# Attention denominators inverted on gpsimd, as a power of minus one, in place of VectorE's reciprocal

## The reference, cut to what matters

```python
scores = einsum('bmhd,bnhd->bhmn', q, k) / sqrt(2)        # head width 2
scores = where(scores >= 0, scores, 0.2 * scores)
beta = softmax(scores, axis=-1)
out = einsum('bhmn,bnhd->bmhd', beta, v)                  # value width 16
x = xn + (gamma * out + xn) + experts(xn)                 # 12 MLP experts, top 2 of 16
```

## Time and profile before

| | us |
|---|---|
| median of 3 runs (941.28 to 942.41) | 942.19 |
| profiled execution, first to last instruction | 940.0 |
| DVE busy in it | 735.3 (78%) |
| PE busy | 861.2 (92%) |
| ACT busy | 691.3 (74%) |
| POOL busy | 601.5 (64%) |
| first attention stretch (about) | 127 to 365 |
| experts (about) | 365 to 541 |
| second attention stretch (about) | 541 to 936 |

### The profile page before, as it was taken

One profiled execution on the slowest core, in us unless ns is written; L12 is line 12 of the kernel. 1 busy time (PEld: TensorE's weight loads), 2 busy tenths in 40 slices (PEclk: granted clock), 3 DMA queues, 4 the chain that ended last, 5 costly groups with the idle time before them and its releaser, 6 DMA issues. The chain is left out here.

```text
span 940.0 us, 20061 instructions
## 1 busy us (share of the span) xinstructions
PE 861.2 (92%) x7499; PEld 348.9 (37%) x7500; DVE 735.3 (78%) x859; ACT 691.3 (74%) x811; POOL 601.5 (64%) x610
## 2 busy tenths in 40 slices
PE   0688269999999999999999999999999999999997
PEld 0444112222222224776867732222222222222222
DVE  5788889999999994101011099999999999999996
ACT  0578888888888887444453568888888888888886
POOL 3355247777777663999999226657567575765782
PEclk9999659999999999999999999999999999999999
DMA  7833101111111112233242210102112111210202
GB/s 214 303 66 74 32 27 33 51 40 51 47 27 36 25 38 88 90 121 116 93 138 71 94 44 22 40 19 59 36 25 59 25 36 29 70 29 13 69 18 55
DMA packets 71225, 59.36 MB, mean 63 GB/s; under 512 B 33770, under 2 KB 58178, under 8 KB 71136
## 3 DMA queue, kind: packets, MB, share of 16 engines
q1 hardware_dynamic: 61520, 48.06, 17.6%
q0 software_dynamic: 8192, 9.37, 3.6%
q10 hardware_dynamic: 1424, 0.76, 0.3%
HBM read 31.58 MB, written 30.02 MB: 66 GB/s over the span
## 5 line engine op out<-in xcount | busy, mean ns | idle before, releaser
L1133 DVE TENSOR_SCALAR ps<-ps 128x1024 f32<-128x1024 f32 x512 | 600.1, 1224 | 14.6 <-PE ps L825 11.7
L718 ACT ACTIVATE pr<-ps 128x1024 f32<-128x1024 f32 x512 | 523.4, 1023 | 104.5 <-PE ps L835 72.9
L855 PE MATMUL ps<-pr,vp 128*32 128x256 f32 x4096 | 327.2, 392 | 0.1
L835 PE MATMUL ps<-q,kz 64*128 64x512 bf16 x1024 | 200.7, 389 | 10.2 <-DVE ps L1133 4.4
L825 PE MATMUL ps<-q,kz 62*128 62x512 bf16 x1024 | 200.3, 389 | 2.9 <-DMA q<-parts_dram 1.3
L505 POOL DMA_INDIRECT xs<-eout,idxs x128 | 129.0, 1008 | 105.0 <-ACT pr L718 75.5
L490 POOL DMA_INDIRECT disp<-xn,idx x128 | 125.9, 984 | 50.8 <-issue 29.2
L835 PEld LDWEIGHTS ps<-q,kz 64*128 64x128 bf16 x1024 | 49.0, 93 | 225.7 <-DVE ps L1133 188.4
L1152 DVE TENSOR_TENSOR pr<-ps,parts 128x1024 f32<-128x1024 f32 x12 | 14.7, 1225 | 149.6 <-PE ps L920 149.6
L855 PEld LDWEIGHTS ps<-pr,vp 128*32 128x32 f32 x4096 | 81.1, 108 | 119.4 <-issue 117.6
L744 ACT ACTIVATE pr<-ps,b1s 128x512 f32<-128x512 f32 x96 | 65.8, 687 | 53.7 <-PE ps L909 53.7
(11 more groups left out here) (122 smaller groups left out, 530.3 us busy)
## 6 DMA issues: line engine op xcount, KB each, us to landing
moved<-att SPq DMA_DIRECT2D x480, 8.0 KB
disp<-pr SPq DMA_DIRECT2D x12, 512.0 KB, 4.9
eout<-pr SPq DMA_DIRECT2D x12, 512.0 KB, 2.9
y<-in_x SPq DMA_DIRECT2D x8, 512.0 KB, 8.1
out<-y SPq DMA_DIRECT2D x7, 512.0 KB
w<-in_w1t SPq DMA_DIRECT2D x12, 256.0 KB, 3.2
w<-in_w2t SPq DMA_DIRECT2D x12, 256.0 KB, 3.4
xs<-disp SPq DMA_DIRECT2D x6, 512.0 KB, 4.9
```

The lines of the kernel that those rows point to most:

```text
L718: act.activation(pr[:, c % BUFS, 2 * pair:2 * pair + 2, :], ring[i % RING], ACT.Exp, scale=SLOPE).then_inc(S["exps"], 1)
L835: last = pe.matmul(ring[i % RING][:, k, :], kz[r:r + TILE, hg, pair, kc * P:(kc + 1) * P], q2[r:r + TILE, hg, qh * HALF:(qh + 1) * HALF], ...
L855: last = pe.matmul(acc[p % 2][32 * g:32 * g + 32, cols], vp[:, hg, kc, g, :], pr[:, c % BUFS, g % PAIRS * 2 + g // PAIRS, cols], start=(kc ...
L1133: dve.tensor_scalar(s, s, 0.0, 1.0 / SLOPE - 1.0, ALU.max, ALU.mult).then_inc(S["relu"], 1)
```

## The change

DVE no longer runs `denominators`. POOL's `quotient(p)` waits for the transpose itself (`turned`), raises the 16 denominators of each partition to the power of minus one, taken from a tile that is filled once with -1, waits for its own result, and then multiplies as before. The reciprocal in `finish` stays on DVE with a semaphore of its own, and stands behind the wait for `y_att` instead of ahead of it.

```diff
+        minus = sb("minus", [P, HALF // BLOCK])
...
+            pool.memset(minus[:], -1.0)
...
             def quotient(p):
-                pool.wait_ge(S["rg_rdy"], p + 1)
+                pool.wait_ge(S["turned"], p + 1)
+                rows = ot[:, p % 2, :].rearrange("p (q c) -> p q c", c=BLOCK)
+                pool.tensor_tensor(rg[:, p % 2, :], rows[:, :, DV], minus[:], ALU.pow).then_inc(S["rg_rdy"], 1)
+                pool.wait_ge(S["rg_rdy"], quotients(p))
...
-            def denominators(p):
-
-                dve.wait_ge(S["turned"], p + 1)
-                rows = ot[:, p % 2, :].rearrange("p (q c) -> p q c", c=BLOCK)
-                dve.reciprocal(rg[:, p % 2, :], rows[:, :, DV]).then_inc(S["rg_rdy"], 1)
...
             def finish(p):
...
-                dve.reciprocal(inv_rows, rows[:, :, :, DV]).then_inc(S["rg_rdy"], 1)
-                dve.wait_ge(S["rg_rdy"], p + 1)
                 dve.wait_ge(S["y_att"], p - 1)
+                dve.reciprocal(inv_rows, rows[:, :, :, DV]).then_inc(S["rg_last"], 1)
+                dve.wait_ge(S["rg_last"], 1 + LAST.index(p))
...
-                    if i % UP == TURN + 1 and i > first + UP:
-                        denominators(i // UP - 1)
```

More of the change, by code:

```diff
@@ L202, in build @@
                  "qz_init weighted at_rdy sum_rdy inv_rdy row_step route ones_rdy max_rdy off_rdy reset_rdy r_exp cnt_rdy pos_rdy ztile init_rdy kz_init "
-                 "ld0 ld1 vp_rdy s1 relu s2 exps pv acc_evac o_rdy turned rg_rdy att_rdy spread0 spread1 y_att "
+                 "ld0 ld1 vp_rdy s1 relu s2 exps pv acc_evac o_rdy turned rg_rdy rg_last att_rdy spread0 spread1 y_att "
                  "scat staged pool_step carry "
```

## The result

| | before | changed |
|---|---|---|
| median of the runs, us | 941.74 | 985.26 |
| profiled span, us | 940.0 | 985.5 |
| first rectify of pass 1, and of pass 11 (first stretch) | 147.97, 342.25 | 148.07, 342.29 |
| first unit of the first expert on PE | 363.17 | 382.18 |
| first rectify of pass 12, and of pass 31 | 540.83, 911.87 | 564.98, 935.89 |

The ratio is 1.047 (95% interval 1.046 to 1.049): 43.5 us slower by the medians, where 0.8 us was predicted and 950 us was the upper end of the range. The two profiled executions, from which all rows come, differ by 45.5 us. The attention passes themselves are as long as before. The time stands in two places: 24 us between the first stretch and the second, and another 21 us behind the loop, at the end.

A forecast was written before the change was run, and what follows sets the result against it. It took PE's round through ACT, two units in 2.40 us, to set the pace. Span 940.0 - 1.3 (loop) + 2.0 (last two quotients) = 940.7; with medians 2.2 above the span, 943.0 us, range 940.2 to 950.0.

The forecast's parts named there:

- The price of the power: POOL's power of 128x16 in each quotient: 0.8 us, taken between 0.25 and 1.6.
- X: Time added on POOL per quotient, power plus wait for its own result: 1.0 us (0.4 to 1.8).
- 3X - 2.3: Move of the kernel's end with a dear power, once POOL's cover at 900.59 is used up; X = 2.5 gives 947.4.
- POOL's waits for ACT: POOL's idle time in the attention stretches hides X: 17.7 us in the first, 75.5 us in the second.
- the cover of the experts' loads: First expert's loads have some 8 us of cover; delay counts from X of about 2.3, at 11 us per further us.
- The end itself: POOL's chain at the kernel's end: nothing hides the last two quotients, which add 2X = 2.0 us.
- The cover of 0.97 us at 900.59: POOL's wait near the end: the third-last quotient adds only what exceeds 0.97 us, nothing with X = 1.0.
- the 0.09 us per second pass: Attention passes with a load wait at a new half of heads: 0.09 saved for about 15 passes, 1.3 us.
- Rival 1: The power on POOL is dear, X above 1.4: slower, 944.4 at X = 1.5, 951 at X = 2.6; chance 0.33.
- rival 2: POOL overrun, X of 4 or more: 30 quotients exceed its idle time, 965 us or far above; chance 0.06.
- Rival 3: The reciprocal's whole time comes back in the attention loop: gain 4.6 us, end 939.7 with X = 1.0; chance 0.09.
- Rival 4: POOL's chain at the end isn't the one that counts: 940.9 us; chance 0.04.

The follow-up runs named there:

- tail: Kernel before, DVE's reciprocal kept, POOL also forming the power for the last two quotients only (passes 29 and 30): 947.76 us, ratio 1.0076.
- q28b: Kernel before, reciprocal kept, POOL also forming the power for pass 28 only, run once more: 947.38 us in its one execution.
- short: Kernel before, reciprocal kept, ACT's exponentials over 448 of each 512 columns: 924.00 us, ratio 0.9805.
- short_none: Kernel before with exponentials over 448 of 512 columns, and neither reciprocal nor power in 30 of 32 passes: 922.17 us, ratio 0.9791.
- vbf16: Kernel before with exponentials and values held in bf16 for the values matmuls, no work left out: 924.02 us, ratio 0.9814.
- both: Kernel before, DVE's reciprocal kept, POOL forming the power too, into a spare tile: 986.71 us, ratio 1.0487.
- none: Kernel before with neither reciprocal nor power in 30 of 32 passes, POOL multiplying by ones: 940.99 us, ratio 0.9993.

## Why the prediction was wrong, step by step

**The price of the power failed, and with it the forecast.** The prediction took 0.8 us between 0.25 and 1.6. It carried DVE's ratio per element (5.6) over to POOL, where 158 ns stand against 1.55, a hundredfold, and took an indirect DMA as the nearest row from above, which has nothing to do with arithmetic. The power measured 2.94. The upper bound should have been called unknown: the text said that a power could be dearer, then cut the range as if it could not.

**The warning was there.** The selection rule that the prediction quoted from the Trainium skill (GPSIMD Engine Reference, Engine selection) speaks against the move, rightly. Its factor of two stands there for adding, multiplying and maxima; carried over to the power it gave 0.47 us, and that is off by six. The trace decides: 2.94 us.

**The price of what follows was mis-sized too.** For X = 3.0 the prediction's own formula gives 3X - 2.3 = 6.8 and 11 times 0.7, so 957 us; 985 were measured. Three steps of it failed, and a fourth term was missing.
1. It read POOL's waits for ACT as slack: 17.7 us in the first stretch, 75.5 in the second. With 33 us of powers in the first stretch and more, the idle time ahead of its scatters went only from 50.8 to 46.1 us, and ahead of the gathers from 105.0 to 66.4. A gap of 0.30 us between two indirect DMAs, and 0.97 behind an addition, stands whatever the profile names as the releaser: gaps of 0.3 us stand ahead of 109 of the 128 scatters of the changed kernel and of 106 of the 128 gathers. What shrank, and so could be used, was 4.7 us in the first stretch and 38.6 in the second.
2. It put the cover of the experts' loads at about 8 us and at the scatters. The loads moved by 25.2 us (352.12 to 377.34) and PE by 19.0, so the cover was 6.2, and what held them was the spread of pass 9, ahead of them on SP's queue, which starts with POOL's quotient. The prediction had looked at the spread behind them.
3. It said that in the middle of the second stretch nobody waits for X, and let only three quotients count. What POOL can't catch up adds up until the end: 17 quotients of the second stretch come before that of pass 29, 51 us of powers, and 16.7 us of it was still there (19.7 less that quotient's own 3.0).
4. It had no term for TensorE's clock. The two waits of PE at the experts cost 3.3 us beyond themselves, at a granted clock of 0.50.

**The end itself was right.** That the last two quotients count in full was shown by `tail`. The prediction calls them those of passes 45 and 46; the kernel has 32 passes, and they are 29 and 30 (and 28 where it says 44). The cover of 0.97 us at 900.59 failed (`q28b`).

**DVE's side was right in kind.** A reciprocal of 0.15 us effective on an engine that is busy 99% was worth nearly nothing, for the reason given: two units take 2.40 us through ACT and PE, whatever DVE saves in one is lost in the next. `short`, `short_none` and `vbf16` show that this round set the pace. What failed is the 0.09 us per second pass, which should have hidden behind ACT. Shifted pairs of the changed kernel, at the boundary of two halves of the heads (timeline, PE):

```profile
642.58 0.39 PE L840 MATMUL ps<-q,kz 64*128 64x512 bf16 x2
...
643.71 0.39 PE L840 MATMUL ps<-q,kz 64*128 64x512 bf16 x2
...
645.07 0.39 PE L840 MATMUL ps<-q,kz 64*128 64x512 bf16 x2
...
646.18 0.39 PE L840 MATMUL ps<-q,kz 64*128 64x512 bf16 x2
```

The phase did change, the steps are 1.13, 1.36, 1.11. At the turn they are 1.43 and 1.13 (L840 at 631.54, 632.97, 634.10), as forecast. But at the boundary the long step has 0.09 more all the same (1.36 for 1.27), so the pass is 19.46 again and the gain is 0.1 us per stretch, not 1.3 in all. Even this 0.1 is not shown to be the reciprocal's: `both` keeps it and has the same 349.59 us. Nor is it shown that the 0.09 is a wait for the load, as the prediction has it: SP issued the last load of that half at 617.91, 26 us ahead of the scores behind 643.71, and no row of the loop names a load as what PE waited for.

**Rivals.** Rival 1 named the mechanism and had 0.33; rival 2, POOL overrun, had 0.06 and gave its point as X of 4. The point from which POOL falls behind lies below 1.0 us. Rival 3 (all of DVE's time comes back) is refuted by `none` and shown to be right only for a kernel with a shorter round. Rival 4 is refuted by `tail`.

## What to carry to other kernels

An operation that no row of the trace shows on that engine has no upper bound: measure it first, in a corner of the kernel where the engine is idle, before moving it. Idle time of an engine is slack only where it shrinks when the engine is late; gaps of one size ahead of one kind of instruction are its own cost, whatever releaser stands beside them. An engine can be busy 99% and not set the pace: follow one instruction from unit to unit, and where two steps always sum to the same, look for the round that makes them.

## What the hardware showed

A power on GpSimd costs 158 ns per element of a partition (0.55 us for 1, 1.01 for 4, 2.9 for 16, 10.5 for 64), whatever base, exponent or stride, where a product of 16 takes 0.21 us. Behind a power the next gather is dearer by some 0.2 us with its gap (1.40 against 1.20 behind a fill). After a standstill of 19 us TensorE was granted 0.50 of its clock (1.2 GHz), and eight transposes took 1.94 us instead of 1.09. Cutting a values group of PE in two made the unit 0.15 us longer (1.35 against 1.20), though the columns were the same. The values of 256 columns take 4096 matmuls of 392 ns in fp32, and 2048 of 287 ns in bf16.
